# Graph layer with attention and experts on one core: the steps of a node tile follow each other twice a place instead of once

## What is computed

```
xn  = layernorm(x)
nb  = segment_sum(edge_weight * xn[src], dst)              # neighbour sums
gnn = leaky(xn @ W1.T + b1 + (nb + nb*xn) @ W2.T + b2);  gnn /= norm(gnn)
kv  = einsum(k, v) / N          # k, v: per-head layernorms of xn @ w_qkv
mix = gelu((q @ kv + xn) @ w1 + b1) @ w2 + b2 + xn
x1  = x + gnn + mix
h   = layernorm(x1)
idx, prb = argmax and max of softmax(h @ gate_w + gate_b)  # 8 experts
pos = place of the node among those of its expert          # a running count
y   = (relu(h @ w1[idx] + b1[idx]) @ w2[idx] + b2[idx]) * prb   # if pos < capacity
out = x1 + y
```

## Time and profile before

| | us |
|---|---|
| median of 3 runs | 3226.21 |
| lowest, highest | 3226.19, 3241.27 |
| the profiled execution, time | 3227.74 |
| its span in the trace | 3226.0 |
| TensorE busy | 2391.7 (74%) |
| GpSimd busy | 1931.6 (60%) |
| VectorE busy | 1537.6 (48%) |
| ScalarE busy | 932.3 (29%) |
| mean granted clock of TensorE | 0.874 of full |

### The profile page before, as it was taken

One profiled execution on the slowest core, in us unless ns is written; L12 is line 12 of the kernel. 1 busy time (PEld: TensorE's weight loads), 2 busy tenths in 40 slices (PEclk: granted clock), 3 DMA queues, 4 the chain that ended last, 5 costly groups with the idle time before them and its releaser, 6 DMA issues.

```text
span 3226.0 us, 40169 instructions
## 1 busy us (share of the span) xinstructions
PE 2391.7 (74%) x11900; PEld 1748.9 (54%) x11900; DVE 1537.6 (48%) x4468; ACT 932.3 (29%) x2125; POOL 1931.6 (60%) x1905
## 2 busy tenths in 40 slices
PE   0277777765677778887788887777778678588998
PEld 0134444433555556665566665556556456477887
DVE  7466666652465555554344344344344344344222
ACT  4122222211333434332232232223232222232332
POOL 0466666666666666666666666666666666623332
PEclk9999999987788878888989888898888788798999
DMA  9644444434454565555555555555554554535663
GB/s 284 189 134 137 133 139 134 134 113 121 145 151 145 155 202 157 168 170 153 173 171 164 168 172 153 161 166 163 155 158 121 168 147 125 166 99 156 185 182 98
DMA packets 361873, 501.49 MB, mean 155 GB/s; under 512 B 58585, under 2 KB 289487, under 8 KB 361553
## 3 DMA queue, kind: packets, MB, share of 16 engines
q0 software_dynamic: 101376, 243.85, 28.2%
q1 hardware_dynamic: 219394, 216.65, 21.3%
q10 hardware_dynamic: 40886, 38.41, 3.6%
HBM read 436.45 MB, written 66.01 MB: 156 GB/s over the span
## 4 chain that ended last, share of the span: by engine, by line
PE 43%; another core or an unknown queue 22%; issue 14%; DVE 10%; ACT 7%; DVEq 2%; DMA 1%; ACTq 1%; SPq 0%; POOL 0%; POOLq 0%
PE bank L903 9%; PE bank L922 9%; PE bank L735 6%; PE bank L765 5%; PE bank L808 2%; PE bank L820 2%; PE bank L825 2%; PE bank L823 2%; DVEq L1125 1%; PE bank L744 1%; PE bank L869 1%; DVE arena L1142 1%; PE bank L763 1%; ACT L1526 1%
## 5 line engine op out<-in xcount | busy, mean ns | idle before, releaser
L677 POOL DMA_INDIRECT rows_sb<-xn_scratch,src_sb x1664 | 1638.6, 985 | 954.2 <-issue 554.7
L735 PE MATMUL bank<-rows_sb,s_sb 128*48 128x256 f32 x3328 | 466.0, 408 | 159.6 <-issue 83.6
L903 PE MATMUL bank<-acc 128*128 128x256 f32 x1792 | 469.6, 409 | 33.5 <-issue 20.2
L922 PE MATMUL bank<-acc 128*128 128x256 f32 x1792 | 466.5, 405 | 30.7 <-issue 17.0
L735 PEld LDWEIGHTS bank<-rows_sb,s_sb 128*48 128x48 f32 x3328 | 218.0, 129 | 363.4 <-issue 227.2
L922 PEld LDWEIGHTS bank<-acc 128*128 128x128 f32 x1792 | 362.2, 206 | 96.6 <-issue 25.4
L903 PEld LDWEIGHTS bank<-acc 128*128 128x128 f32 x1792 | 359.9, 205 | 95.6 <-issue 45.7
L1554 ACT ACTIVATE acc<-bank,acc 128x256 f32<-128x256 f32 x448 | 187.8, 471 | 521.2 <-PE bank L903 255.1
L703 POOL DMA_INDIRECT out_dram<-acc,sca_i x112 | 179.5, 1603 | 256.0 <-DVE acc L1350 228.5
L1480 ACT COPY sums<-bank 112x256 f32<-112x256 f32 x208 | 77.5, 372 | 791.6 <-remote 704.5
L808 PE MATMUL bank<-arena,weff 128*128 128x128 f32 (+1 forms) x784 | 145.5, 343 | 129.0 <-issue 70.4
(11 more groups left out here) (208 smaller groups left out, 3425.9 us busy)
## 6 DMA issues: line engine op xcount, KB each, us to landing
acc<-ffn_w_in SPq DMA_DIRECT2D x112, 1024.0 KB
rows_sb<-xn_scratch,src_sb POOLq DMA_INDIRECT x1664
arena<-xn_scratch SPq DMA_DIRECT2D x194, 128.0 KB
xnt_scratch<-arena SPq DMA_DIRECT2D x97, 128.0 KB
arena<-xnt_scratch SPq DMA_DIRECT2D x97, 128.0 KB
arena<-x_in SPq DMA_DIRECT2D x97, 128.0 KB
h_scratch<-arena ACTq DMA_DIRECT2D x97, 128.0 KB
out_dram<-arena ACTq DMA_DIRECT2D x97, 128.0 KB
```

Of the source, the lines that this page charges most:

```text
L677: pool.indirect_dma_start(out=rows_sb[:, c % ROW_SLOTS, :], out_offset=None, in_=xn_d, in_offset=bass.IndirectOffsetOnAxis(ap=src_sb[:, c: ...
L735: m = pe.matmul(psum[0][i * HALF:i * HALF + WIN, 0:D], s_sb[:, p % S_SLOTS, i * GROUP + j, :], rows_sb[:, c % ROW_SLOTS, :], start=j == 0, ...
L903: m = pe.matmul(bank[:, i * UNIT:(i + 1) * UNIT], w1_sb[k % 2][:, h, f * P:(f + 1) * P], xt[:, k % 2, h, :], start=h == 0, stop=h == H - 1)
L922: m = pe.matmul(bank[:, i * D:(i + 1) * D], hid[:, f, i * P:(i + 1) * P], w2_sb[k % 2][:, f, :], start=f == 0 and i == 0, stop=f == FC - 1 ...
```

## The change

Steps are counted in half places, here called *half-ticks*: half-tick 2p is ahead of place p's first unit tick, 2p + 1 behind it. Step s of a tile is at half-tick `2 * enters[t] + s`, so that a tile takes 4.5 places and not 9. The turned load is issued at step -2, the row loads at step 0 (before: at steps 0 and 2), the load into the accumulator at step 3 as before. The batches follow: choosing is at half-tick `2 * enters[last] + 8`, sums two half-ticks on, rank three, building two (and three for the tiles behind the fourth), tables one behind building, slots two behind the last building. Tiles 43 to 97 enter one place later than before, the first 43 at the same place. The cost model that places unit ticks and the numbers for loads, gathers and scatters count in half of the new numbers. The core of the diff:

```diff
-            ready = min((groups_before(t) - 1) // 2, PAIRS - 2)
+            ready = min((groups_before(t) + 1) // 2, PAIRS - 1)
...
-        chosen_at = [enters[v[-1]] + C_STEPS - 1 for v in routes]
+        chosen_at = [2 * enters[v[-1]] + C_STEPS - 1 for v in routes]
...
-            found = [("logit", t) for t, e in enumerate(enters) if e + 8 == p]
+            found = [("logit", t) for t, e in enumerate(enters) if 2 * e + 8 == tick]
             for b in range(len(routes)):
-                if chosen_at[b] + 1 == p:
+                if chosen_at[b] + 2 == tick:
                     found.append(("sums", b))
-                if chosen_at[b] + 2 == p:
+                if chosen_at[b] + 3 == tick:
                     found.append(("rank", b))
-            tiles = [t for t in range(T) if build_at[t] + 1 == p]
+            tiles = [t for t in range(T) if build_at[t] + 1 == tick]
...
-        last_c = slots_at[-1]
-        for p in range(FIRST_C, last_c + 1):
-            at_place(p).append(("early", p))
-            at_place(p).append(("late", p))
+        last_c = slots_at[-1] // 2
+        for tick in range(2 * FIRST_C - 2, slots_at[-1] + 1):
+            at_place(tick // 2).append(("tick", tick))
...
-                wanted = slots_at[b] + (4 if slots_at[b] + 4 < PAIRS else 2)
+                wanted = slots_at[b] // 2 + (4 if slots_at[b] // 2 + 4 < PAIRS else 2)
...
-        def c_steps(p, order):
-            return [(enters.index(p - s), s) for s in order if p - s in enters]
+        def c_steps(tick, order):
+            return [(enters.index((tick - s) // 2), s) for s in order if (tick - s) % 2 == 0 and (tick - s) // 2 in enters]
```

On SyncE:

```diff
-                        for t, s in c_steps(k, (2, 0, 3)):
-                            if s == 0:
+                        for t, s in c_steps(k, (0, -2, 3)):
+                            if s == -2:
                                 load_turned(t)
-                            elif s == 2:
+                            elif s == 0:
                                 load_rows(t)
```

On TensorE:

```diff
-                elif kind == "early":
+                elif kind == "tick":
                     small_products(k)
-                    for t, s in c_steps(k, (7,)):
-                        c_step(t, s)
-                elif kind == "late":
-                    for t, s in c_steps(k, (1, 3)):
+                    for t, s in c_steps(k, (7, 3, 1)):
                         c_step(t, s)
```

More of the change, by code:

```diff
@@ L405, in small_steps @@
             for b in range(len(routes)):
-                if slots_at[b] == p and units_after(b) > units_after(b - 1):
+                if slots_at[b] == tick and units_after(b) > units_after(b - 1):
                     found.append(("slots", b))
             return found
-        last_c = slots_at[-1]
-        for p in range(FIRST_C, last_c + 1):
-            at_place(p).append(("early", p))
-            at_place(p).append(("late", p))
+        small_steps = [small_of(tick) for tick in range(slots_at[-1] + 1)]
+        last_c = slots_at[-1] // 2
+        for tick in range(2 * FIRST_C - 2, slots_at[-1] + 1):
+            at_place(tick // 2).append(("tick", tick))
         PE_PLACE, PE_EXPERT = 10.0, 2.7
@@ L439, in build @@
                 time += PE_PLACE - (2.9 if p < PAIRS else 0.0)
-                time -= sum(v for s_, v in PE_STEP.items() if p - s_ in enters)
+                time -= sum(v for s_, v in PE_STEP.items() for i in range(2) if (2 * p + i - s_) / 2 in enters)
             e_place.append(p)
@@ L443, in build @@
             here = at_place(e_place[n])
-            after = next((i for i, v in enumerate(here) if v == ("late", e_place[n])), len(here))
+            after = next((i for i, v in enumerate(here) if v == ("tick", 2 * e_place[n] + 1)), len(here))
             if ("unit", n - 1) in here or after == len(here):
@@ L456, in build @@
         for k in range(K):
-            known = slots_at[batch_of[k]] + 1
+            known = slots_at[batch_of[k]] // 2 + 1
             w1_at[max([known] + [place_of(k - 1, 0)] * (k > 1))].append(k)
@@ L840, in small_products @@
             def small_products(p):
-                steps = small_steps(p)
+                steps = small_steps[p]
                 if not steps:
@@ L1119, in add_group @@
                     k = loaded[0] - LAP_TILES
-                    assert enters[k] + 4 < min(g // 2 + 2, PAIRS), (g, k)
+                    assert enters[k] + 3 < min(g // 2 + 2, PAIRS), (g, k)
                     dve.wait_ge(acc_ld[k % len(acc_ld)], 16 * (k // len(acc_ld) + 1))
@@ L1404, in table_group @@
             def table_group(t):
-                return sum(1 for p in range(FIRST_C, build_at[t] + 2) if small_steps(p))
+                return sum(1 for steps in small_steps[0:build_at[t] + 2] if steps)
             def build_table(t):
@@ L1501, in logit_group @@
             def logit_group(t):
-                return sum(1 for p in range(FIRST_C, enters[t] + 9) if small_steps(p))
+                return sum(1 for steps in small_steps[0:2 * enters[t] + 9] if steps)
             def c_step(t, s):
```

2 lines of the change are left out of this document (1 added, 1 removed).

## The result

The changed kernel takes 3263.06 us (median of 5 runs, 3254.93 to 3272.21) beside 3231.05 us of the kernel before (5 runs, 3226.19 to 3241.27). The ratio is 1.0095, with a 95% interval of 1.0067 to 1.0124. The forecast was 3246 with a range of 3190 to 3288, and slower by over 0.5% as the likeliest case. Against the forecast of +20 us over the median the measured change is +32.

The account below looks back on a forecast made before the run. GpSimd's gathers plus release set 11.9 us a place until the last pair, then TensorE bounds. Terms 11 + 5 + 59 - 12 - 17 - 27 = +19 on the profiled 3227.74 give 3247; median forecast 3246, range 3190 to 3288.

Parts of the forecast that it names:

- GpSimd's transfers: Pair phase: two more units gathered and two more scattered by the last pair, +11 us (7 to 13).
- Batch places: Places with sums, rank and tables together: waits for VectorE delay the next pair, +59 us (18 to 95); old batch costs go, -12.
- rival C: VectorE's 18 us in a batch's place run over into the next, 3 us in all eighteen: 3300 us; chance 0.12.
- Every step in one place: Dense places 51 to 93 without a batch: steps 7, 3, 1 make a longer chain, +5 us (0 to 17).
- more even places: Step 1 moves to the lighter place, so TensorE's excess over 11.9 us falls from 1.5 to 0.7: -17 us (-33 to -8).
- The tail: Behind the last pair: one unit less -14, shorter TensorE waits -10, clock -3; together -27 us (-37 to -14).
- The ScalarE chain: Dense places: table load and root end 1.98 us behind the release, without the skill's further 1380 ns of draining.
- Rival A: Batch waits are covered by slack of products ready before their release: batch term about 5, time 3191 us; chance 0.18.
- however early TensorE was: Pair phase, undisturbed places: the release comes about 1.9 us behind the last gather's issue, whenever TensorE finished the pair.

Follow-up runs that it names:

- all-spaced kernel: Changed kernel with sums, rank and tables of all 20 batches one place apart again: 3213.46 us, ratio 0.9996; on another chip 3211.55 us, ratio 1.0007.
- the one with eighteen batches spaced: Changed kernel with the eighteen batches ahead of the last pair spaced one place apart, the last two not: 2838.12 us, ratio 0.9961; on another chip 3204.18, 0.9986.

## Why the prediction was right

The steps of the prediction, beside the profiled executions.

1. **GpSimd's transfers: +11 forecast, +10.9 in the floors.** Right.
2. **Batch places: +59 - 12 = +47 forecast, +49.9 measured.** Right in sum. The six batches of seven tiles were put at 5 each; five had 5.0 to 6.2, the sixth 1.2 since it fell on a place with two gathers. The others were put at 2.4 and had 3.1. The parts were off in both directions: the new excess is 78.7 us and not 59, 66.8 in the places of the sums and 11.9 in the two behind each, and the old one was 28.8 and not 12. That VectorE's long place runs over into the next (rival C) can be no more than these 11.9 us, under a quarter of the 54 that C took, and before the change the same places had 21.
3. **Every step in one place: +5, more even places: -17; together -12 forecast, +3.3 measured.** This step failed in sign, by 15 us. It is the second term that failed: in the dense part the excess outside batches went from 2.2 us to about zero, and in the later places, where 17 us were to be gained, it rose from 23.6 to 29.0. The rows of TensorE's work in a place were right, but the places outside the batches are late less by their work than by a release that is held, of a relu's product for one. At place 122 of the changed kernel, the first layer's products, ScalarE's relu of them and the second layer's products:

```profile
1711.58 1.91 PE L903 MATMUL bank<-acc 128*128 128x256 f32 x8
```

```profile
1731.68 0.47 ACT L1550 ACTIVATE acc<-bank,acc 128x256 f32<-128x256 f32 x1 [12.86 <-remote]
```

```profile
1732.58 3.78 PE L922 MATMUL bank<-acc 128*128 128x256 f32 x8 [6.12 <-ACT acc L1550]
```

The products end at 1713.5 by their record and ScalarE is released at 1731.7, 18 us later (it stood idle for 12.9 of them), so TensorE stands 6.1 us, and the pair behind it makes the place last 20.5 us. GpSimd had issued transfers without a pause from 1705.9 on, and the release came 3.4 us behind the end of the last one:

```profile
1727.29 0.95 POOL L677 DMA_INDIRECT rows_sb<-xn_scratch,src_sb  x1 [0.30 <-issue]
1738.91 0.94 POOL L677 DMA_INDIRECT rows_sb<-xn_scratch,src_sb  x1 [10.67 <-PE bank L735]
```

The prediction knew of held releases, but priced them as a fixed 1.9 us behind the last gather and for the pair alone. Three places over 4 us make 21.7 of the changed kernel's 29.0 us outside the batches; in the later run of the all-spaced kernel seven make 47.2 where the sum is 42.6, since its other places lie a little under the floors. Held releases stand in all three of the changed kernel: at place 113 the same relu is released 13.9 us behind the products' modelled end. For the seven of the other run it is not shown.

The ScalarE chain was priced by its rows, too, and at this place the activation again starts 0.02 us behind its table load's end, so the further 1380 ns of the Trainium skill ("ScalarE: Activation LUTs", "What ACT_TABLE_LOAD costs") are not seen in the changed kernel either:

```profile
1717.23 1.28 ACT L1522 ACT_TABLE_LOAD   x1
1718.53 0.29 ACT L1522 ACTIVATE c_rstd<-c_stat,eps_sb 128x1 f32<-128x1 f32 x1
```

4. **The tail: -27 forecast, -28.2 measured** from the last pair's copy on. Right, and so are its parts: the unit less is 14.3 us of it by the rows of its ticks, as forecast; TensorE's waits fell by 12.5 (22.1 to 9.6), 10 were forecast; the wait for a unit's gather fell from 6.3 to 1.6 and was not quite gone. The 1.4 that remain stand where 3 were put for the clock, which rose from 0.87 to 0.90 in the stretch with pauses. The quick last two batches are worth 7.6 us behind the last copy, by the run that spaces them (354.7) against the one that doesn't (347.1) on one chip.

The sum, +19, stands against +27 between the profiled spans (3226.0 and 3253.0) and +32 between the medians; the profiled execution of the changed kernel is the shortest of its five, so 5 us have no place in this account. Up to the last pair's copy +46 were forecast and +55.2 came: 10.9, 49.9 and 3.3 as above, 1.6 ahead of place 51, and -10.4 between GpSimd's first gather for the last pair and its copy. For these last three places the prediction had no term. So the tail is right by its mechanism, and a part of the nearness is luck: the 15 us of the third step were in good part made up by 10 that nobody forecast.

**Rival A** ("the batch waits are covered", 3191) was dismissed because all small products are released with the pair. That holds only where releases are held. On the chip without them the changed kernel's loss is zero, and most of the batch waits are covered as A had it: place 62 takes 10.1 us, where the median of its like there is 10.25, and of eighteen such places three are clearly longer than theirs (by 2.9, 7.7 and 4.2 us). But the batch term is not gone: over these medians the places at a batch have 25.8 us in the changed kernel and 14.5 in the one with eighteen batches spaced, so the quick batches cost some 11 us there against the spaced ones, and 48 to 56 with held releases. The kernel before has no profile on this chip, so its own term is not known. The statement that the release comes "however early TensorE was" was read as a rule of the kernel; it is one of three of the four chips.

## What to carry to other kernels

Before steps of a serial chain between engines (sums, rank, table) are put into one slot of a pipeline, ask what else the same in-order queue has to issue behind them: here each round trip to VectorE delayed the next pair's products, and the pacing engine waited. Keep a round trip a slot apart while the pipeline runs, and pull it together only at its end, where nothing queues behind; the kernel that does both has the lowest ratios measured. Only on the chip without held releases is it clear of the kernel before (0.9961, 0.9948 to 0.9974); with them it is 0.9986 (0.996 to 1.0013), apart neither from it nor from the kernel with all batches spaced. Repeat a comparison on a second chip before a mechanism is called the kernel's own.

## What the runs showed of the hardware that was not expected

**Releases of TensorE can be held for many microseconds on some chips, while GpSimd issues indirect transfers back to back.** The kernel before and after wait for "remote" there, a release that the trace can't match with the product's end. ScalarE's waits for the pair from 1190 us on, in the changed kernel on the first chip:

```profile
ACT sums L1476 <- remote: 421.1, 64, 15.8
...
ACT sums L1476 <- PE bank L735: 73.8, 32, 12.9
```

and the same kernel on the chip that takes 2848 us for it, from 1190 to 2480 us:

```profile
ACT sums L1476 <- PE bank L735: 498.8, 107, 13.9
ACT acc L1550 <- PE bank L903: 207.3, 108, 4.5
```

There the trace names the product for each of these waits. A pair's products, and then the copy:

```profile
708.17 1.93 PE L735 MATMUL bank<-rows_sb,s_sb 128*48 128x256 f32 x16
```

```profile
710.15 0.37 ACT L1476 COPY sums<-bank 112x256 f32<-112x256 f32 x1 [1.25 <-PE bank L735]
```

0.05 us from the modelled end to the copy, against 6.5 in the earlier trace rows; and GpSimd mostly goes from pair to pair without a wait, here to the gather at 704.40, the first of its pair. It paused for over 0.4 us ahead of 5 of the 156 pairs counted above, and in the kernel before, with held releases, ahead of 133:

```profile
703.12 0.97 POOL L677 DMA_INDIRECT rows_sb<-xn_scratch,src_sb  x1 [0.30 <-issue]
704.40 0.95 POOL L677 DMA_INDIRECT rows_sb<-xn_scratch,src_sb  x1 [0.30 <-issue]
705.65 0.95 POOL L677 DMA_INDIRECT rows_sb<-xn_scratch,src_sb  x1 [0.30 <-issue]
```

The instructions themselves last the same, 0.95 us. So a place without unit transfers takes 10.2 us there (median) and 11.9 to 12.0 elsewhere, and the kernel 2849 us and not 3209 to 3231.

**Where releases are held, they come when GpSimd pauses.** In the kernel before, 133 of the 190 copies in places 10 to 199 start over 1.5 us behind their product's modelled end. For 126 of them the release falls in a pause of GpSimd of more than 0.4 us, with a median of 1.6 us behind the end of its last transfer (the middle half 1.4 to 1.9); in the changed kernel it is 122 of 128, with the same median. This is the fixed lag behind the last gather that the prediction took for the pace, and it would explain why an early product gained nothing: its release waited for the pause that GpSimd makes when it has run out of buffers. That the pause itself brings the release is the nearest reading of these times; no run put a pause in to try it.

That the holding needs GpSimd's dense stream is supported by the run with half the gathers (median lag 0.05 on a chip where the spaced kernel has 1.9 to 2.7), and that it isn't the data by the run with half the rows. What holds the release, and why one chip does not, is open.
